# Six instead of eleven instructions in the state's split into pieces, on the steps whose product uses three of its six kinds

## What is computed

```
def cell(h, x):
    gi = x @ W_ih + b_ih
    gh = h @ W_hh + b_hh
    r = sigmoid(i_r + h_r); z = sigmoid(i_z + h_z)
    n = tanh(i_n + r * h_n)
    h_new = (1.0 - z) * n + z * h
...
_, hs = jax.lax.scan(cell, initial_state, xs)      # 64 steps, one after the other
x = x + ffn(hs)                                    # quantised gate, up and down products
```

## Time and profile before

| | |
|---|---|
| median of three runs | 2879.51 us (2878.58 to 2880.59) |
| profiled execution, its span | 2879.2 us; its own time is not listed apart, the median of the runs lies 0.3 us above the span |
| TensorE, matmul | busy 89% of the span |
| VectorE | busy 59% |
| GpSimd / ScalarE | busy 44% / 40% |
| mean granted TensorE clock | 0.96 of full speed |

### The profile page before, as it was taken

How to read it: one execution, slowest core, us unless ns; L and a number is a source line. 1 busy time by engine, 2 the same in 40 slices (tenths; PEclk the granted TensorE clock), 3 DMA queues, 4 the chain that set the end, 5 groups by cost and what they waited for, 6 DMA issues and landing times. The chain is left out here.

```text
span 2879.2 us, 154632 instructions
## 1 busy us (share of the span) xinstructions
PE 2562.9 (89%) x67605; PEld 1681.0 (58%) x67605; DVE 1685.2 (59%) x3398; ACT 1140.6 (40%) x2317; POOL 1262.3 (44%) x598
## 2 busy tenths in 40 slices
PE   2088999998889999999999999999996999999995
PEld 1066777776768888887675564655642444444442
DVE  8852222225632222225646778867592888888887
ACT  1321222225632222224702333323232777777773
POOL 0255666662046666664061363622700333333334
PEclk8599999999999999999999999999998999999998
DMA  6833222224422222226554253442432223232322
GB/s 193 239 85 77 74 73 71 73 71 112 131 63 71 74 73 70 73 71 167 152 135 127 92 151 118 115 156 85 129 143 93 74 84 95 84 95 84 95 63 53
DMA packets 234843, 293.74 MB, mean 102 GB/s; under 512 B 69581, under 2 KB 194023, under 8 KB 233895
## 3 DMA queue, kind: packets, MB, share of 16 engines
q1 hardware_dynamic: 212743, 240.84, 30.6%
q10 hardware_dynamic: 18304, 36.19, 3.6%
q0 software_dynamic: 3680, 15.21, 1.9%
HBM read 231.61 MB, written 60.45 MB: 101 GB/s over the span
## 5 line engine op out<-in xcount | busy, mean ns | idle before, releaser
L1145 PE MATMUL psum<-second_shared 64*32 64x384 f16 x32768 | 1026.0, 324 | 50.2 <-issue 31.3
L1153 PE MATMUL psum<-low_w,low_hot 64*32 64x384 f16 x16384 | 756.5, 324 | 2.0 <-issue 2.0
L1372 DVE TENSOR_SCALAR second_shared<-psum 32x384 f16<-32x384 f32 x496 | 272.3, 549 | 749.1 <-PE psum L1145 741.9
L953 POOL TENSOR_TENSOR low_hot<-first_shared,sum_mask 128x1024 f16<-128x1024 f16 x256 | 499.8, 1952 | 430.1 <-DVE first_shared L1359 183.8
L1145 PEld LDWEIGHTS psum<-second_shared 64*32 64x32 f16 x32768 | 561.5, 93 | 198.0 <-issue 89.8
L947 POOL TENSOR_TENSOR second_shared<-first_shared,whole_mask 128x2048 f16<-128x2048 f16 x128 | 462.5, 3614 | 460.1 <-PE psum L1145 348.2
L1044 ACT ACTIVATE second_shared<-psum 32x384 f16<-32x384 f32 x496 | 239.8, 483 | 801.9 <-PE psum L1145 795.9
L1233 PE MATMUL psum<-low_w,low_hot 64*64 64x384 f16 x12288 | 513.7, 326 | 19.9 <-issue 13.5
L1233 PEld LDWEIGHTS psum<-low_w,low_hot 64*64 64x64 f16 x12288 | 378.3, 108 | 150.4 <-issue 18.4
L310 PE MATMUL psum<-w_x,x_cols 128*64 128x512 f32 (+1 forms) x1856 | 312.0, 495 | 9.5 <-ACT x_cols L280 9.5
L1153 PEld LDWEIGHTS psum<-low_w,low_hot 64*32 64x32 f16 x16384 | 282.5, 93 | 56.8 <-issue 3.1
(11 more groups left out here) (286 smaller groups left out, 2746.6 us busy)
## 6 DMA issues: line engine op xcount, KB each, us to landing
low_w<-w_rows SPq DMA_DIRECT2D x384, 144.0 KB
low_w<-w_rows SPq DMA_DIRECT2D x256, 120.0 KB
second_shared<-w_rows SPq DMA_DIRECT2D x1024, 24.0 KB, 1.9
x_gates<-x_out ACTq DMA_DIRECT2D x58, 384.0 KB, 2.3
xg<-x_gates SPq DMA_DIRECT2D x58, 384.0 KB, 3.2
low_w<-w_rows SPq DMA_DIRECT2D x256, 72.0 KB
low_w<-w_rows SPq DMA_DIRECT2D x384, 48.0 KB
w_rows<-quantised SPq DMA_DIRECT2D x24, 384.0 KB, 4.9
```

Of the source, the lines that this page charges most:

```text
L953: nc.gpsimd.tensor_tensor(low_hot[:, buf].rearrange("p (s k) b -> p s k b", s=SUBS), low_a[:, slot, bass.ds(c, 1), :, :].rearrange("p a s ...
L1145: last = nc.tensor.matmul(run[m][u][j * Q:(j + 1) * Q, :], whole_hot[rows[u], m, sign, kk, j % 2 * Q:(j % 2 + 1) * Q], whole_w[rows[u], m, ...
L1153: nc.tensor.matmul(run[m][u][j * Q:(j + 1) * Q, :], low_hot[rows[u], m, kk, j % 2 * Q:(j % 2 + 1) * Q], low_w[rows[u], m, at:at + UC], sta ...
L1372: last = nc.vector.tensor_scalar(whole_w[u * B:u * B + Q, m, 0, bq, :], run[m][u][bq * Q:(bq + 1) * Q, :], 1.0 / HIGH_ONE, None, ALU.mult)
```

## The change

A second helper `cut_for_sums` makes only A0, A1H and A2H, by the first six instructions of `cut`, which are the same. Steps 2 to 5 use it. The semaphore `cut_h`, which counted 11 for each step, now counts 11 for step 1 and 6 for each later one; `cuts_by` gives the sum. Steps 0 and 1 and the cuts of the input keep all eleven. The pieces A1, A2 and A3 of the state are no longer written in steps 2 to 5.

```
+            def cut_for_sums(v, link, src, unit, rest, rest_h, piece):
+
+                vt, vs = nc.vector.tensor_tensor, nc.vector.tensor_scalar
+                yield link(vs(rest, src, unit, None, ALU.mult))
+                yield link(vs(piece[A0], rest, GRID_ONE, GRID_ONE, ALU.add, ALU.subtract))
+                yield link(vt(rest, rest, piece[A0], ALU.subtract))
+                yield link(nc.vector.tensor_copy(piece[A1H], rest))
+                yield link(vt(rest_h, rest, piece[A1H], ALU.subtract))
+                yield link(nc.vector.tensor_copy(piece[A2H], rest_h))
+
+            CUTS, SUM_CUTS = 11, 6
+
+            def cuts_by(t):
+
+                return CUTS * min(t, FINE - 1) + SUM_CUTS * max(0, t - FINE + 1)
...
                             pe.wait_ge(state_ok, t)
-                            need(pe, cut_h, CUTS * (t - 1))
+                            need(pe, cut_h, cuts_by(t - 1))
...
                         def pick(t):
-                            pe.wait_ge(cut_h, CUTS * t)
+                            pe.wait_ge(cut_h, cuts_by(t))
...
-                            for _ in cut(v, link, ps_a_both.rearrange("p (j s b) -> p s j b", j=2, s=2), scale[:, 3:4],
+                            for _ in (cut if t < FINE else cut_for_sums)(v, link, ps_a_both.rearrange("p (j s b) -> p s j b", j=2, s=2), scale[:, 3:4],
```

More of the change, by code:

```diff
@@ L231, in cut @@
                 yield link(nc.vector.tensor_copy(piece[A3], rest))
-            CUTS = 11
+            def cut_for_sums(v, link, src, unit, rest, rest_h, piece):
[9 more added lines that the diff above has]
+                return CUTS * min(t, FINE - 1) + SUM_CUTS * max(0, t - FINE + 1)
             PIECES_OUT = 16 * A_KINDS
@@ L1334, in cut_state @@
                         def cut_state(t):
-                            n = [CUTS * (t - 1)]
+                            n = [cuts_by(t - 1)]
                             def link(ins):
@@ L1348, in cut_state @@
                                 pass
-                            assert n[0] == CUTS * t
+                            assert n[0] == cuts_by(t)
                         def place_second(t):
```

## The result

The changed kernel took **2864.18 us** in the median of four runs (2859.2 to 2867.96) and the kernel before 2879.05 us (2877.49 to 2880.59, four runs). The ratio is 0.9949 with an interval of 0.9935 to 0.9963, so the change is worth 10.7 to 18.7 us. The forecast was 2870.0 with a range from 2866.5. It is faster, as forecast, and by more than forecast.

A forecast was written before the change was run, and what follows sets the result against it. The prediction took TensorE to set the pace, idling in steps 2 to 5 for VectorE's cut. Cuts 7.6 us plus pick clock 1.9 made 9.5 us off 2879.5, so 2870.0 us, range 2866.5 to 2874.2.

The forecast's parts named there:

- Five instructions fewer in each cut: In the cuts of steps 2 to 5, the picks' wait ends 1.90 us sooner each, 7.6 us in all.
- Nothing hides the cut, and nothing behind ends at a time of its own: In steps 2 to 5 all later work needs the cut and TensorE sets the pace, so earlier starts mean earlier ends.
- TensorE's clock in the picks: In the picks of steps 2 to 5, less low-clock time saves 1.9 us, with ends -2.9 and +8.2.
- the second case: Around the picks, low stretches become 3.42 us: three steps save 2.3 us, step 2 another 1.7, together 4.0.
- The clock elsewhere: Slower rival: longer low stretches at `x_window` cost 6.8 us, with pick losses 11.4, giving 2883.3 us; chance 0.04.
- The open gate: Rival: in all four steps' picks the clock stays high and all 8.2 us return, 2863.7 us; chance 0.10.
- Given back by VectorE in step 5: Rival: VectorE's quantised-weight instructions in step 5 are held up, up to 7.9 us back, 2873.9 to 2877.9 us; chance 0.13.

The follow-up runs named there:

- the run with two steps: Kernel before with six cut instructions in steps 4 and 5 only, eleven in steps 2 and 3; 2872.94 us, ratio 0.9975 to the kernel before.
- the fourth profile: One more profile of the changed kernel, with no edit; its single run took 2864.04 us.
- filling: Matmuls of zeros in TensorE's idling before the picks: 24 in the kernel before, 2864.43 us; 12 in the changed kernel, 2859.74 us.

## Why the prediction was right and where it was wrong

**Five instructions fewer in each cut: 7.6 us.** Right to the tenth: 19.93 to 12.29 us over four steps. The idling is 2.16 us in steps 3 to 5, as forecast, and 2.70 or 2.83 in step 2, where 2.70 was forecast. The distance between the starts of two equal casts was the right price.

**Nothing hides the cut, and nothing behind ends at a time of its own.** Right. The products, the gates and the loads moved with it; the run with two steps showed about half the gain.

**TensorE's clock in the picks: 1.9 us.** This is the step that failed: the mechanism was right, and the term of the sum was mis-sized. It measured 4.0 us (36.99 to 33.03 in the means). The prediction named two cases, low stretches of 6.83 us (-2.9) and of 3.42 us with no drop in step 2 (+4.0), held the second for the nearer, and then took half of it. The runs show the second case almost as written. The low time in the picks of steps 3 and 5 of the first profile is 2.7 to 2.8 us where 2.65 and 3.17 were computed, and in three of four profiles step 2's picks had none. The first two stretches of picks in the fourth profile, steps 2 and 3, show it: the one is 7.09 us at clock 1.00, and the other keeps its low part, as steps 4 and 5 do:

```profile
1428.55:1435.64 7.09, 7.09 (x64) 6.17 (x65) 5.66 (x14) 5.28 (x14) 4.46 (x3) 1.00 0.17 42
1612.42:1620.84 8.42, 8.42 (x64) 6.85 (x64) 5.75 (x14) 5.27 (x14) 4.95 (x3) 0.84 0.01 3
```

That it comes to the 4.0 of the second case so closely is in part luck. The first two profiles alone give 2.3 us (36.3 to 34.0), as in that profile of the changed kernel step 2's picks still had 2.8 us of low clock. And the 3.42 us that the prediction read in step 2 was one execution's: in the two later profiles of the kernel before, that low stretch was 6.83 us, with 4.5 and 4.8 us of it in the picks.

With 4.0 in place of 1.9 the sum would have been 2879.5 - 11.6 = 2867.9, still inside the range. The next term did the rest.

**The clock elsewhere: taken at nothing on the good side.** The prediction priced a low stretch at the start of `x_window` only as a loss. In step 3 it was a gain in three of four profiles of the changed kernel (`x_window` 0.9 us in the mean). With the products' 1.0 us, which is not shown to belong to the change, that makes the 13.4 us of the stages, and a time of about 2866, just outside the range. The four runs of the result then lie 2.2 to 2.7 us under the two later medians of the same kernel (2866.4 and 2866.9), which is within how its executions differ (2857 to 2873). The range was too narrow for both: three runs within about 2 us had made the kernel look steadier than it is.

**The open gate** (2863.7 us, chance 0.10) gave nearly the measured time by a wrong mechanism: the clock still dropped 1.43 us into the idling in step 3, and 4.7 us were still lost in the picks on average. By filling, the last gap before the picks became 0.2 us (0.8 in step 2), and the clock stayed high in all four pick stretches. By that, the advice of the Trainium skill ("TensorE: Matmul & The Clock Gate", section "HAM oscillation — how this bites in real kernels") to keep gaps short holds in its direction, though half the old gap was not yet short enough here.

**Given back by VectorE in step 5** did not happen here (4.9 us before, 5.0 after in two waits). The mechanism is real, as the kernel with its last five instructions behind the placing showed.

## What to carry to other kernels

An instruction that only one other engine's wait covers is worth its start-to-start distance each time; take that from two equal instructions in the trace. Where TensorE idles behind such a wait, add the time that its next work spends at the low clock, and when the rows leave two cases, let the range reach past the better one too. Before moving work "off the path", look at which engine is running there: beside GpSimd's products VectorE's instructions of 0.3 to 0.4 us took up to 2 us.

## What was not expected of the hardware

- Five instructions that cost 1.90 us with GpSimd idle took 4.0 to 6.7 us beside it, and the products grew by 18 us over four steps.
- Low stretches of the clock around the picks lasted 6.83 us in steps 3 to 5 in all three profiles of the kernel before and 3.41 us in all four of the changed one, whose idling is 1.90 us shorter. With five instructions more they lasted 10.24, 6.83 and 10.24 us.
- 24 matmuls of zeros in the idling of four steps, with no useful result, made the kernel before 15.5 us faster, a little more than the change itself did (13.1 to 14.9).
- The same program spread over 12 us in 12 runs, and a stretch that no edit touched differed by up to 12 us between the profiles of all kernels (1419.7 to 1431.7 us).
